# Last attention's hop layer: the position term as a second accumulating product, gelu read from PSUM

## The reference, cut to what matters

```
pp = pos_phases[:L]                                        # 750 x 32, the same for all 8 batches
off_in = jnp.concatenate([x, jnp.broadcast_to(pp[None], (B, L, P))], axis=-1)     # 64 + 32 features
ao = (gelu(off_in @ hop_w1 + hop_b1) @ hop_w2 + hop_b2).reshape(B, L, H, P + 1)
...
ctx = jnp.cumsum(x @ kce_w + kce_b, axis=1)
storage_in = jnp.concatenate([x, ctx / pos], axis=-1)
st_ph = jnp.tanh(gelu(storage_in @ ksk_w1 + ksk_b1) @ ksk_w2 + ksk_b2) * PI
gate = jax.nn.sigmoid(gelu(x @ sg_w1 + sg_b1) @ sg_w2 + sg_b2)
```

## Time and profile before

| | |
|---|---|
| median of 3 runs (lowest, highest) | 1339.23 us (1338.63, 1341.33) |
| the profiled execution's own time | 1339.48 us |
| its span, first to last instruction | 1337.6 us |
| busy: PE, PEld, DVE, ACT, POOL | 1221.2, 789.4, 776.2, 641.5, 527.1 us |
| mean granted TensorE clock | 0.912 |
| last attention with its `hidden` events | about 944 to 1230 us of the span |

### The profile page before, as it was taken

The page is one execution under the profiler, slowest core; times in us unless marked ns, Lnnn a source line. Parts: engine busy times, 40 slices in busy tenths (PEclk is TensorE's granted clock), DMA queues, the critical chain, the costliest instruction groups (busy, mean ns, idle before and its releaser), DMA issues.

```text
span 1337.6 us, 27027 instructions
## 1 busy us (share of the span) xinstructions
PE 1221.2 (91%) x10203; PEld 789.4 (59%) x10203; DVE 776.2 (58%) x1724; ACT 641.5 (48%) x1372; POOL 527.1 (39%) x1111
## 2 busy tenths in 40 slices
PE   6989999999999999999999997799708889889998
PEld 4755665666666666666666664545305676675553
DVE  3545555655556566565565661143677898985542
ACT  1236555555555554555555553050255664744564
POOL 3111454754554644545455444306871020421200
PEclk9979999999999999999999999799757667568999
DMA  4100000000000000000000001102110000000001
GB/s 84 18 5 2 2 3 2 4 6 2 4 2 2 3 2 2 2 2 2 3 2 3 2 2 32 62 34 48 17 14 1 1 1 1 13 1 0 13 12 23
DMA packets 34076, 14.57 MB, mean 11 GB/s; under 512 B 30738, under 2 KB 31346, under 8 KB 33949
## 3 DMA queue, kind: packets, MB, share of 16 engines
q1 hardware_dynamic: 29341, 10.95, 3.6%
q0 software_dynamic: 4608, 1.91, 1.5%
HBM read 6.46 MB, written 7.27 MB: 10 GB/s over the span
## 4 chain that ended last, share of the span: by engine, by line
PE 70%; DVE 11%; POOL 6%; issue 5%; ACT 4%; SPq 2%; DMA 1%; POOLq 0%; DVEq 0%; ACTq 0%
PE psum L755 20%; PE psum L736 10%; PE psum L664 8%; PE psum L727 7%; PE psum L711 4%; POOL XN L1311 3%; PE psum L1008 2%; PE psum L649 2%; DVE arena L1979 2%; PE psum L988 1%; PE psum L809 1%; PE psum L822 1%; PE psum L1023 1%; PE psum L688 1%; SPq L1094 1%
## 5 line engine op out<-in xcount | busy, mean ns | idle before, releaser
L1429 ACT ACTIVATE arena<-psum 125x500 f32<-125x500 f32 x576 | 307.0, 585 | 329.8 <-PE psum L736 329.8
L1780 DVE TENSOR_REDUCE arena<-psum 125x1 f32<-125x500 f32 x384 | 242.5, 674 | 199.9 <-PE psum L664 199.8
L664 PE MATMUL psum<-arena 32*125 32x500 f32 (+1 forms) x1536 | 322.4, 516 | 0.3 <-ACT arena L1420 0.3
L755 PE MATMUL psum<-arena,XN 125*64 125x250 f32 x2304 | 307.4, 387 | 0.2 <-ACT arena L1429 0.2
L736 PE MATMUL psum<-arena 32*125 32x250 f32 x2304 | 291.7, 370 | 0.0
L736 PEld LDWEIGHTS psum<-arena 32*125 32x125 f32 x2304 | 214.6, 183 | 11.8 <-issue 1.0
L755 PEld LDWEIGHTS psum<-arena,XN 125*64 125x64 f32 x2304 | 140.2, 136 | 121.2 <-issue 78.4
L1783 DVE TENSOR_REDUCE arena<-psum 125x2 f32<-125x500 f32 x192 | 121.3, 674 | 71.1 <-PE psum L664 66.9
L664 PEld LDWEIGHTS psum<-arena 32*125 32x125 f32 x1536 | 126.4, 183 | 3.7 <-DVE arena L1780 1.0
L727 PE MATMUL psum<-arena,onesb 3*125 3x500 bf16 x576 | 122.4, 422 | 2.1 <-DMA arena<-arena 2.1
L1204 POOL TENSOR_TENSOR lnst<-lnst,mhalf 125x12 f32<-125x12 f32 x14 | 32.0, 2286 | 231.3 <-DVE lnst L1759 231.3
(11 more groups left out here) (343 smaller groups left out, 1948.7 us busy)
## 6 DMA issues: line engine op xcount, KB each, us to landing
arena<-arena SPq DMA_DIRECT2D x192, 1.5 KB
expert_in<-XN SPq DMA_DIRECT2D x8, 256.0 KB, 4.8
arena<-expert_in SPq DMA_DIRECT2D x4, 512.0 KB, 5.3
expert_out<-arena SPq DMA_DIRECT2D x4, 512.0 KB, 3.1
out<-H SPq DMA_DIRECT2D x16, 93.8 KB
expert_in<-XN,slot_in POOLq DMA_INDIRECT x48
XN<-expert_out,slot_out POOLq DMA_INDIRECT x48, 3.8
arena<-in_L_ffn_w SPq DMA_DIRECT2D x2, 256.0 KB
```

Source lines behind the costliest of these rows:

```text
L664: last = pe.matmul(ps[0:R, at_:at_ + hi - lo], QH[row:row + 32, b, g, j * R:(j + 1) * R], KH[row:row + 32, b, g, lo:hi], start=True, stop= ...
L755: last = pe.matmul(ctx_bank[64 * h2:64 * h2 + 64, 0:THIRD], XN[:, p, c, a, :], PR[:, x % 4, h2, i * THIRD:(i + 1) * THIRD], start=(c == 0) ...
L1429: act.activation(PR[:, x % 4, h2, :], st_bank[(2 * x + h2) % 3][0:R, 0:2 * THIRD], ACT.Exp)\
L1780: dve.reduce_max(MX[:, q % 2, 0, 2 * h2 + tile:2 * h2 + tile + 1], ps[0:R, 0:2 * THIRD], AX)\
```

## The change

The sum of the two terms is made in PSUM. After each `hop` product of `XT` PE adds a product of 32 rows, `hop1b[0:32]` with `ppt`, into the same bank; ACT takes the gelu straight from the bank with the bias `hopb`, and frees it. DVE's `hop_hidden` (8 adds), `PPF` and what made it (two products on PE, two activations on ACT in the convolution stage) are gone. `ppt` and `hop1b` now live to the end: `ppt` gets a buffer of its own and `hop1b` moves from the arena to the buffer `wall` of weights. PE's `tokens` waits for the two `hop` banks instead of the semaphore `hop_act`.

```diff
@@ weights and buffers
-                 ("hopb", 1), ("rb1", 1), ("lng", 1), ("lnb", 1)]
+                 ("hopb", 1), ("rb1", 1), ("lng", 1), ("lnb", 1), ("hop1b", 128)]
-        ppt, at = view(at, [NJ * R], parts=PP)
-        early = [("hop1b", 128), ("kskb", 128), ("kcet", 128), ("kce", 64), ("kb1", 1), ("kceb", 1)]
+        early = [("kskb", 128), ("kcet", 128), ("kce", 64), ("kb1", 1), ("kceb", 1)]
-        PPF = sb("PPF", [128, L])
+        ppt = sb("ppt", [PP, L])
@@ PE, after convolution 6
-                    emptied(pe, ("ppt", 0))
-                    emptied(pe, ("ppt", 1))
-                    for h in range(2):
-                        ps, done = take(pe, ("ppf", h))
-                        pe.matmul(ps[:, 0:HALF], W["hop1b"][0:PP, :], ppt[:, h * HALF:(h + 1) * HALF],
-                                  start=True, stop=True).then_inc(done, 1)
@@ PE, hidden(p)
                         ps, done = take(pe, (name, p, th))
-                        pe.matmul(ps[0:w.shape[1], 0:HALF], w, XT[:, cols], start=True, stop=True).then_inc(done, 1)
+                        last = pe.matmul(ps[0:w.shape[1], 0:HALF], w, XT[:, cols], start=True, stop=(name == "sg"))
+                        if name == "hop":
+                            last = pe.matmul(ps[:, 0:HALF], W["hop1b"][0:PP, :], ppt[:, th * HALF:(th + 1) * HALF],
+                                             start=False, stop=True)
+                        last.then_inc(done, 1)
@@ PE, tokens(p, h)
-                    pe.wait_ge(S["hop_act"], 2 * (p + 1))
+                    for th in range(2):
+                        emptied(pe, ("hop", p, th))
@@ ACT, after convolution 6
-                    for h in range(2):
-                        ps, done = filled(act, ("ppf", h))
-                        act.activation(PPF[:, h * HALF:(h + 1) * HALF], ps[:, 0:HALF], ACT.Identity, bias=W["hopb"])\
-                           .then_inc(done, 1)
@@ ACT, hidden(p)
-                    emptied(act, ("hop", p, th))
-                    act.activation(HG[:, own], HG[:, own], ACT.Gelu).then_inc(S["hop_act"], 1)
+                    ps, done = filled(act, ("hop", p, th))
+                    act.activation(HG[:, own], ps[:, 0:HALF], ACT.Gelu, bias=W["hopb"]).then_inc(done, 1)
@@ DVE
-            def hop_hidden(p):
-                for th in range(2):
-                    ps, done = filled(dve, ("hop", p, th))
-                    own = slice(p % 2 * L + th * HALF, p % 2 * L + (th + 1) * HALF)
-                    dve.tensor_tensor(HG[:, own], ps[:, 0:HALF], PPF[:, th * HALF:(th + 1) * HALF], ALU.add)\
-                       .then_inc(done, 1)
-                elif kind == "hidden":
-                    hop_hidden(x)
```

## The result

The changed kernel takes 1344.87 us (median of 11 runs, 1341.81 to 1347.10), the kernel before 1339.23 (11 runs): ratio 1.0039, 95% interval 1.0029 to 1.0049, so 5.6 us slower. The forecast was 1341.0, the range 1337.3 to 1343.8. The profiled execution took 1343.06 us with a span of 1341.2.

What follows compares the result with a forecast made beforehand. PE was taken to bound the kernel, holding 70% of the chain that ended last. Start -0.63, second pair +0.53, third +0.62, fourth +1.30 made +1.82 us, so 1341.0 us, range 1337.3 to 1343.8.

Steps and rivals of the forecast that it cites:

- The start: Convolution stage: without PE's two products L603, L1723 moves forward by its 0.67 us idle less 0.04: 0.63 us gained.
- rival 2: The clock falls in the convolutions, before convolution 8, where PE idles 0.97 us: +3.5 us, time 1342.7, chance 0.13.
- First pair: First hop layer: PE's added 1.30 us is covered by DVE's late token reading and ACT's 1.88 us idle: 0.
- DVE's lag as the only gain: Behind the hop layers, dropping DVE's adds gains at most its lag behind PE: 0.77 us second pair, 0.68 third, fourth none.
- The added product: PE's hop layer: each added product costs 0.65 us in both halves, whatever its rows, so 1.30 us a pair.
- that moment: The clock's rise inside `hidden` keeps its time, so a product ahead of it pushes equal work across, costing 0.65 us.
- Rival 1: `hidden`, pairs two to four: clock rises one product later, first half's product 1.35 us: +3.92, time 1343.1, chance 0.17.
- a `hidden` 2 us longer: Sign on PE that the half-clock price carries; the forecast itself had `hidden` longer by 1.3 us a pair.
- Rival 3: Sixth token tile, second and third pair: a shorter PE gap keeps the clock: -1.4 us, time 1337.8, chance 0.10.
- Gelu from PSUM, bank waits: On ACT the gelu takes 564 ns instead of 516, covered; PE's bank waits before the tokens are long fulfilled: cost 0.

Runs made afterwards that it cites:

- the second profile: The changed kernel run once more, unaltered, for another profile: 1344.47 us in one run.
- the fill: Kernel before plus unread products of 128 rows and 384 columns in PE's idle time ahead of the features: 1338.83 us, ratio 1.0000.

## Why the prediction was wrong, step by step

- **The start: right.** L1723 (now L1717) without idle time, the stage 0.64 us earlier (forecast 0.63), PE's idle 0.96 (0.97), PEclk 1.00 over 46 to 52 us: rival 2 did not come. Whether the 0.64 us survive to the end was not shown: where the first attention begins, at 101 us, the profiles of all these kernels lie between -1.4 and +2.3 us of before, by when the clock happens to rise at 95 to 100 us.
- **First pair: right, 0.** The layer is 2.2 us longer, and the stages behind it moved by 0.13 us, forward. (In the second profile they moved forward by 0.84, but so they did in a profile of the kernel before with the fill, which keeps the adds.) DVE still takes its token tiles without a wait.
- **DVE's lag as the only gain: right.** Of the 2.31 and 3.34 us that PE lost, 0.71 and 0.68 were covered by it; the forecast had 0.77 and 0.68. In the fourth pair nothing, as forecast.
- **The added product: wrong twice.** The step was "The number of rows makes no visible difference. [...] I take 0.65 for both halves". At full clock it costs 0.82 us; L603's 0.73 was nearer. Three pairs: 6 x 0.17 = +1.0 us. The larger error was "if that moment stays where it is in time". It did not: the rise came 1.4, 3.5 and 0.9 us later behind the layer's start. Taking the 1.64 us of length from 2.31, 3.34 and 2.03 leaves 0.67, 1.70 and 0.39: 2.76 us by the clock. That fits the delays, since work done at half clock takes twice its time: half of them is 0.72, 1.75 and 0.43. Length and clock make 3.8 us; the 0.25 us that came back at the sixth token tile, less a cover 0.06 smaller than forecast, take it to the 3.6 by which the three pairs missed (6.03 against 2.45).
- **Rival 1 named the right place and direction** (half-clock price, +3.92, 1343.1, chance 0.17), and its sign, a `hidden` 2 us longer, is in the rows; but it was priced as one product at its half-clock length. Measured is a rise 0.9 to 3.5 us later, by up to more than two products at half clock, and a half-clock price of 1.54 instead of 1.35 (`hop`, L850 and `sg` at half clock take 1061.38 - 1056.90 = 4.48 us, the two alone 1061.00 - 1058.06 = 2.94). What I had held against it, that nothing ties the rise to the products, was an argument from missing rows: none of before sets a product of few rows against one of 128 ahead of a rise.
- **Rival 3 came only in a trace of it.** The gap before the second pair's sixth token tile shrank from 3.66 to 3.35 us, not to 2.9, and the tile ran at full clock for its first 0.3 us alone, PEclk 0.56 in the window above against 0.50: 0.25 us instead of 1.6. A gap as short as the one for which the Trainium skill's rule was weighed ("TensorE: Matmul & The Clock Gate", section "HAM oscillation — how this bites in real kernels") did not arise, so no run here shows it at that length.
- **Gelu from PSUM, bank waits: no cost visible.** The gelu, the answer to the earlier trace rows (groups of ACT by form, 938 to 1130 us), takes 573 ns where the forecast had 564, and PE's rows show no wait before the token products (L870 at 1012.20 and 1070.84 above).

```profile
L1492 ACT ACTIVATE arena<-psum,wall 128x375 f32<-128x375 f32 x8 | 4.6, 573 | 6.0 <-PE psum L850 5.9
```

That few rows put off the rise is shown by four pairs of kernels (32 against 128 rows twice, late against early, 64 against 128). Why they do is not: the trace has the granted clock and not what the chip goes by. Open too is why the rise with 128 rows came a little sooner than with no added product (3.6 against 4.3 us), a difference within the scatter of single layers.

## What to carry to other kernels

A product put on a path near a rise of TensorE's clock has two prices, its length and what it does to the rise; price both, and look what rows it has. If a product with few contraction rows must stand there, fill its rows with zeros, or put it behind the rise: here that was worth 5.5 and 2.8 us for no change in the sum. And before moving work into an idle stretch, count the buffers that it holds meanwhile, and ask who empties them.

## What the runs showed of the hardware

- An accumulating fp32 product of 375 columns costs 0.63 us at full clock with 128 rows and 0.82 with 32 rows between products of 128 rows. The Trainium skill ("TensorE: Matmul & The Clock Gate", section "Why this matters for your kernels") says that a single product of 32 rows takes the same time as one of 128. The traces here don't agree: 0.19 us more where the number of rows changes from one product to the next.
- The same product over 32 rows ahead of the rise put it at 5.9 to 8.3 us behind the layer's start, over 128 rows at 2.3 to 4.8. The time of the whole kernel followed, 5.5 and 5.6 us apart.
- PE was busy without a gap and yet stayed at half clock: in the changed kernel's third pair from the features at 1052.16 us to the rise 12.3 us later, in the second profile 12.7 us. In the kernel before it was 8.8 us at the same place.
